# Another order for the first attention: four stages of two key tiles in place of eight of one

## The chip, the cores and the metric

The kernel runs on one core of a Trainium2 chip. The core has TensorE for matrix products (its matmuls are PE in the profile, its weight loads PEld), VectorE (DVE), ScalarE (ACT), GpSimd (POOL) and SyncE (SP, which here issues the DMAs). The engines run side by side, each through its own list of instructions in order, and wait for one another at semaphores. The metric is the device time of one execution in microseconds; lower is better. The median of three runs of the kernel before is 1487.65 us.

## The reference

Two transformer layers over x of shape (2, 1024, 128): a wide attention, a mixture of eight gated experts, a second attention (causal, with a rotary part) and a second mixture. The change is in the first attention:

```python
q = z @ wq @ fcq_w + fcq_b        # 16 heads of 64, z = layernorm(x)
k = z @ wk @ fck_w + fck_b
v = z @ wv @ fcv_w + fcv_b
scores = einsum('bihd,bjhd->bhij', q, k) / 8
attn = softmax(scores, axis=-1)
out = einsum('bhij,bjhd->bihd', attn, v)
return out.reshape(b, n, 1024) @ fco_w + fco_b
```

## The kernel before

The first attention goes through 16 **steps**, numbered 0 to 15. A step handles a pair of heads of one batch. Its 1024 keys are eight key tiles of 128, its 1024 queries two halves of 512. For each key tile `kt` and each half `j` of the queries there is

- a **score unit** (`ST`): four matmuls of 512 columns (L931, L932) that fill one PSUM tile called `pair`; ScalarE turns it into `prob` by an exponential (L680);
- a **value unit** (`PV`, function `product`, L904): the values times `prob`, two fp32 matmuls that the profile shows as four records, summed over the eight key tiles in the PSUM tile `pv`.

GpSimd adds the `prob` of the key tiles up in `psum_k` (L623, L628), for the sums of the softmax. Beside this the step does small jobs, each a letter in the code:

- for the **next** step: `q` twice (the projection of the queries, L854, read by ScalarE at L638 and then by VectorE at L732), `s` sixteen times (the raw scores with queries on the partitions, two matmuls of 64 rows, L863 and L865, of which VectorE takes the maxima at L738), and `m` (the maxima are brought into a row: `mmax` at L742 joins the two halves of the keys, a transpose at L883, then `mrow` at L747, and a DMA from `mrow` into row 0 of the next step's `q2`, L528). The first score unit of a step waits for that DMA (`row_loaded`);
- for the step **before**: `l` (column sums, L888, copied at L751), `r` (reciprocals, L771), `n` (the values times the reciprocals, L775) and `g` (output projection, L893, added at L779).

In steps 0 to 11 a piece of the experts' weights is split as well: VectorE computes two halves of its rest (L812) after all the units of the step and ahead of those of the next one. Steps 12 to 14 carry early parts of the second layer (`R`, `X`, `P`).

All `ST` and all small jobs but `r` and `n` share a ring of three `pair` tiles: a unit on TensorE waits until the tile that was filled three ring places earlier has been read. The order on TensorE, ScalarE and VectorE is the order of `step_script`, which before the change reads the tables `AFTER_SCORES` and `AFTER_VALUES`: for every key tile two `ST`, what the first table says, the two `PV` of the key tile before, what the second table says. So the value units run one key tile behind the scores.

Of the kernel before, what the change touches and what calls it, by code (L numbers as in the profile page):

```python
# [367 lines left out]
def step_units(k_next, k_done):  # L368
# [5 lines left out]

AFTER_SCORES = {
    0: [("q", 0), ("q", 1)],
    1: [("s", 1), ("s", 2)], 2: [("s", 4), ("s", 5)], 3: [("s", 7), ("s", 8)], 4: [("s", 10), ("s", 11)],
    5: [("s", 13), ("s", 14)],
}
AFTER_VALUES = {  # L380
    0: [("s", 0)], 1: [("s", 3), ("l", 0)], 2: [("s", 6), ("X", 0)], 3: [("s", 9), ("r", 0)], 4: [("s", 12)],
    5: [("s", 15)], 6: [("m", 0), ("n", 0), ("R", 0), ("P", 0)], 7: [("g", 0)],
}

# [6 lines left out]
def step_script(n):  # L391

    has = step_units(n + 1 < STEPS0, n > 0) + EARLY.get(n, [])
    out = []
    for kt in range(TT):
        out += [("ST", kt, 0), ("ST", kt, 1)]
        out += [("UNIT",) + u for u in AFTER_SCORES.get(kt, []) if u in has]
        if kt or n:
            out += [("PV", kt - 1, 0), ("PV", kt - 1, 1)]
        out += [("UNIT",) + u for u in AFTER_VALUES.get(kt, []) if u in has]  # L400
    return out
# [45 lines left out]
def l0_attention(nc, m, d):  # L447
    with ExitStack() as ctx:
# [3 lines left out]
        def sem(name):  # L452
            return m.ctx.enter_context(nc.semaphore(name))
# [11 lines left out]
        mx = sb("mx", [P, 2, 2, TT])  # L465
        mmax = sb("mmax", [P, 2, TT])
        tcol = sb("tcol", [2 * TT, P])
# [21 lines left out]
        filled, read = sem("work_filled"), sem("work_read")  # L489
        hi_done, mmax_ready = sem("hi_done"), sem("mmax_ready")  # L490
        st_filled, exp_done, pv_done, ut_ready = sem("st_filled"), sem("exp_done"), sem("pv_done"), sem("ut_ready")
# [20 lines left out]
        def _(sp):  # L512
# [62 lines left out]
            for n in range(STEPS0):  # L575
# [10 lines left out]
                if n:  # L586
                    sums(n - 1, place(n, ("l", 0)))
                if n + 1 < STEPS0:
                    max_rows(n + 1, place(n, ("m", 0)))
                    shift_rows(n + 1)  # L590
            sums(LAST, first_of(STEPS0))
# [40 lines left out]
        def _(act):  # L632
# [27 lines left out]
            for n in range(STEPS0):  # L660
                for what, *rest in step_script(n):
# [3 lines left out]
                    elif what == "PV":  # L665
                        kt, j = rest
                        if kt < 0:
                            keep_product(n - 1, j)
                    else:
# [12 lines left out]
                        if j and kt in (4, 5) and piece_of(n) is not None:  # L682
                            lead_piece(piece_of(n), kt - 4)
                        if j and kt == 2 and n == AT_TURN:

                            act.wait_ge(read, place(PAIRS, ("g", 0)) + 1)
                            act.wait_ge(piece_split, 2 * len(PIECES))
                            nc.scalar.activation(turned[:, :], m.out_t[:, 0:T], ACT.Identity, bias=m.out_bias[:, 0:1]
                                                 ).then_inc(early_act, 1)
                        if j and kt == 6 and n == AT_ROOT:  # L690
                            act.wait_ge(m.aggr_done, NBLK + 2)
                            nc.scalar.activation(m.std0[:, 0:HALF], m.mv[:, 0:HALF, 1], ACT.Sqrt, bias=m.eps[:, 0:1]
                                                 ).then_inc(early_act, 1)
                        if j and kt < 2 and n == AT_LOGITS:

                            act.wait_ge(early_dve, CENTRE)
                            act.wait_ge(read, place(AT_TURN, ("R", 0)) + 1)
                            for t in range(TPB * kt, TPB * (kt + 1)):
# [3 lines left out]
                        if j and kt == 4 and n == AT_LOGITS:  # L702
# [4 lines left out]
                        if j and kt == 0 and n == LAST:  # L707
                            act.wait_ge(early_dve, SHIFTED)
# [6 lines left out]
        def _(v):  # L715
# [8 lines left out]
            def unit(kind, x, u, k):  # L724
# [11 lines left out]
                elif kind == "s":  # L736
                    v.wait_ge(filled, u + 1)
                    nc.vector.reduce_max(mx[:, x % 2, :, x // 2], buf[:, :, :], AX.X).then_inc(read, 1)  # L738
                    if x == S_UNITS - 1:

                        v.wait_ge(read, u + 1)
                        nc.vector.tensor_tensor(mmax[:, :, :], mx[:, 0, :, :], mx[:, 1, :, :], ALU.max  # L742
                                                ).then_inc(mmax_ready, 1)
                elif kind == "m":
                    v.wait_ge(cols_loaded, 16 * (k + 1))
                    v.wait_ge(filled, u + 1)
                    nc.vector.scalar_tensor_tensor(mrow[:, :], buf[0:2 * TT, 0, 0:P], -1.0, tcol[:, :],  # L747
                                                   ALU.mult, ALU.subtract).then_inc(read, 1)
# [96 lines left out]
        def _(pe):  # L845
            def unit(kind, x, u, k):
# [34 lines left out]
                elif kind == "m":  # L881
                    pe.wait_ge(mmax_ready, k + 1)
                    ins = nc.tensor.matmul(buf[0:2 * TT, 0, 0:P], mmax[:, :, :].rearrange("p h t -> p (h t)"),  # L883
                                           m.ident[:, :], start=True, stop=True)
                elif kind == "l":
# [26 lines left out]
            for n in range(STEPS0):  # L912
                for what, *rest in step_script(n):
# [7 lines left out]
                    else:  # L921
# [12 lines left out]
                        ins.then_inc(st_filled, 1)  # L934
            for j in R2:
                product(STEPS0 - 1, TT - 1, j)
            u = first_of(STEPS0)
# [1783 lines left out]
```

## Time and profile before

| | before |
|---|---|
| median of 3 runs | 1487.65 us (1487.17 to 1487.96) |
| the profiled execution | 1486.37 us |
| its span, first to last instruction | 1484.6 us |
| PE busy | 1381.6 us, 93% of the span |
| DVE, ACT, POOL busy | 999.2, 817.5, 863.1 us |
| mean granted clock of TensorE | 0.972 |

The profiled execution is the one that all times of the trace come from; 1.8 us of it lie outside the span. The 16 steps begin at 63.84 us and the last value unit ends at 746.9 us. "Busy" of PE counts matmuls that overlap and have modelled ends, so starts of neighbouring records are a better measure of what a unit costs than the length of one record.

### The profile page before, as it was taken

The numbers are of one execution on the slowest core, as the hardware profiler recorded it, in microseconds if no ns is written. First come the engines' busy times: TensorE is split into PE (matmuls) and PEld (weight loads), VectorE is DVE, ScalarE is ACT, GpSimd is POOL, SyncE is SP. The second block draws the span as 40 slices with busy tenths as digits, with TensorE's granted clock in tenths as the row PEclk, the third lists the DMA queues.
The fourth block names the chain that finished last, engine by engine and source line by source line (L and its number), as shares of the span: only waits on it lengthen the run. The fifth ranks groups of instructions, "written<-read, shape, count | busy, mean of one in ns | idle before, by whom it ended". The sixth has DMA issues, their size and how long they took to land. (4 is left out here: it accounts for less than half of the span.)

```text
span 1484.6 us, 18636 instructions
## 1 busy us (share of the span) xinstructions
PE 1381.6 (93%) x6322; PEld 783.4 (53%) x6322; DVE 999.2 (67%) x1675; ACT 817.5 (55%) x1236; POOL 863.1 (58%) x685
## 2 busy tenths in 40 slices
PE   6699999999999999999978977899999997999998
PEld 5344444444444444544456734454444445787776
DVE  5676777777677777677666678676666725566665
ACT  4244444444444445444545443566776565787776
POOL 0298777777977777787744505455565332344443
PEclk9699999999999999999999997999999998999999
DMA  3110111111011111000050005012111106000000
GB/s 107 33 44 16 58 59 44 58 58 48 26 58 58 51 52 44 15 16 15 26 159 1 1 0 100 15 24 30 21 30 29 30 2 271 1 1 8 8 8 8
DMA packets 32586, 60.59 MB, mean 41 GB/s; under 512 B 9499, under 2 KB 17084, under 8 KB 32348
## 3 DMA queue, kind: packets, MB, share of 16 engines
q1 hardware_dynamic: 32492, 59.40, 14.4%
q8 instruction: 51, 0.84, 0.2%
q14 instruction: 43, 0.35, 0.1%
HBM read 35.13 MB, written 13.89 MB: 33 GB/s over the span
## 5 line engine op out<-in xcount | busy, mean ns | idle before, releaser
L628 POOL TENSOR_TENSOR psum_k<-psum_k,prob 128x1024 f32<-128x1024 f32 x186 | 457.9, 2485 | 46.5 <-ACT prob L680 46.5
L680 ACT ACTIVATE prob<-pair 128x1024 f32<-128x1024 f32 x256 | 250.5, 1025 | 378.7 <-PE pair L932 378.7
L738 DVE TENSOR_REDUCE mx<-pair 128x2 f32<-128x1024 f32 x256 | 305.3, 1222 | 100.0 <-PE pair L865 99.5
L904 PE MATMUL pv<-prob,c_all 128*64 128x512 f32 x1024 | 247.9, 605 | 0.0
L1935 DVE CUSTOM_DVE_ANT_0 l_banks<-l_banks,causal 128x128 f32<-128x128 f32 (+7 forms) x256 | 189.5, 782 | 75.8 <-PE l_banks L1973 74.7
L931 PE MATMUL pair<-qq,ak 128*128 128x512 f32 x512 | 221.5, 433 | 7.1 <-DVE q L732 3.3
L1843 ACT ACTIVATE l_prob<-l_banks 128x1024 f32<-128x1024 f32 (+7 forms) x256 | 155.3, 654 | 111.7 <-PE l_banks L1992 111.0
L932 PE MATMUL pair<-q,kb 128*128 128x512 f32 x512 | 202.4, 395 | 0.0
L2151 POOL TENSOR_TENSOR silu_rest_t<-silu_t,silu_lead_t 128x512 fp32r<-128x512 f32 x74 | 96.4, 1304 | 145.0 <-ACT silu_lead_t L2348 145.0
L1897 POOL TENSOR_SCALAR_AFFINE_SELECT l_prob<-l_prob 128x128 f32<-128x128 f32 x256 | 72.3, 295 | 146.9 <-ACT l_prob L1843 145.3
L623 POOL TENSOR_TENSOR psum_k<-prob 128x1024 f32<-128x1024 f32 x31 | 74.1, 2412 | 118.9 <-ACT prob L680 118.9
L931 PEld LDWEIGHTS pair<-qq,ak 128*128 128x128 f32 x512 | 96.6, 189 | 73.2 <-issue 22.8
L2517 DVE TENSOR_TENSOR silu_t<-silu_t,bank_t 128x512 f32<-128x512 f32 x128 | 88.0, 688 | 64.4 <-ACT silu_t L2339 60.4
L1973 PE MATMUL l_banks<-l_kk,l_qq 128*128 128x512 f32 (+3 forms) x384 | 115.4, 394 | 14.1 <-DMA l_qq<-rounded 4.7
L2339 ACT ACTIVATE silu_t<-bank_t,b_t 128x512 f32<-128x512 f32 x144 | 99.3, 690 | 41.8 <-PE bank_t L951 41.6
L904 PEld LDWEIGHTS pv<-prob,c_all 128*64 128x64 f32 x1024 | 62.1, 136 | 112.6 <-issue 80.6
L863 PE MATMUL pair<-ak,qq 64*128 64x512 f32 x256 | 112.8, 487 | 9.0 <-DVE mx L738 5.0
L1992 PE MATMUL l_banks<-l_qq,l_kk 128*128 128x512 f32 (+3 forms) x384 | 112.1, 385 | 4.2 <-DVE plain L1935 3.2
L865 PE MATMUL pair<-kb,qq 64*128 64x512 f32 x256 | 113.1, 488 | 0.0
L863 PEld LDWEIGHTS pair<-ak,qq 64*128 64x128 f32 x256 | 47.0, 188 | 122.0 <-issue 94.6
L932 PEld LDWEIGHTS pair<-q,kb 128*128 128x128 f32 x512 | 96.9, 189 | 19.8 <-issue 3.3
L1973 PEld LDWEIGHTS l_banks<-l_kk,l_qq 128*128 128x128 f32 x384 | 64.9, 199 | 73.7 <-ACT l_prob L1843 23.6
(318 smaller groups left out, 2276.8 us busy)
## 6 DMA issues: line engine op xcount, KB each, us to landing
plain<-scratch_sums SPq DMA_DIRECT2D x32, 256.0 KB
whole<-in_experts SPq DMA_DIRECT2D x12, 512.0 KB, 5.1
scratch_lead<-rounded SPq DMA_DIRECT2D x12, 512.0 KB, 2.6
scratch_rest<-rounded SPq DMA_DIRECT2D x12, 512.0 KB, 3.9
w_lead_t<-scratch_lead SPq DMA_DIRECT2D x9, 512.0 KB, 6.6
w_rest_t<-scratch_rest SPq DMA_DIRECT2D x9, 512.0 KB, 7.4
l_kk<-rounded SPq DMA_DIRECT2D x16, 256.0 KB, 4.2
l_qq<-rounded SPq DMA_DIRECT2D x16, 256.0 KB, 5.4
```

What stands on the lines that cost most here:

```text
L628: nc.gpsimd.tensor_tensor(total[:, h, :], total[:, h, :], prob[kt % 4][:, h, :], ALU.add).then_inc(summed, 1)
L680: nc.scalar.activation(prob[kt % 4][:, :, ts(j, BLK)], buffer("ST", at)[:, :, :], ACT.Exp, scale=D0 ** -0.5).then_inc(exp_done, 1)
L738: nc.vector.reduce_max(mx[:, x % 2, :, x // 2], buf[:, :, :], AX.X).then_inc(read, 1)
L863: nc.tensor.matmul(buf[:, 0, :], qq[k % 2][0][0:D0, ts(t, P)], m.ak[0:D0, keys], start=True, stop=True)
L865: ins = nc.tensor.matmul(buf[:, 1, :], qq[k % 2][1][D0:P, ts(t, P)], m.kb[D0:P, keys], start=True, stop=True)
L904: ins = nc.tensor.matmul(pv[D0 * h:D0 * (h + 1), ts(j, BLK)], m.c_all[:, TT * (s // PAIRS) + kt, :], prob[kt % 4][:, h, ts(j, BLK)], start ...
L931: nc.tensor.matmul(buf, m.ak[:, keys], qq[n % 2][h][:, ts(j, BLK)], start=True, stop=False)
L932: ins = nc.tensor.matmul(buf, m.kb[:, keys], q2[n % 2][:, h, ts(j, BLK)], start=False, stop=True)
L1843: nc.scalar.activation(prob[kt % 2][:, g, P * kt:T], buffer(item)[:, P * kt - T:], ACT.Exp, scale=SCALE1).then_inc(exp_done, 1)
L1935: ins = nc.vector.tensor_tensor_reduce(scores[:, 0:s_width(t)], scores[:, 0:s_width(t)], hidden, 1.0, -3e38, ALU.add, ALU.max, mx[:, g, t: ...
L1973: ins = nc.tensor.matmul(out[:, lo:end], qq[k % 2][:, g, ts(t, P)], kk[k % 2][:, g, lo:end], start=True, stop=True)
L1992: ins = nc.tensor.matmul(buf[:, at:at + end - lo], kk[n % 2][:, g, ts(kt, P)], qq[n % 2][:, g, lo:end], start=True, stop=True)
```

## The change

One table, `STAGES`, replaces the two. A step is now four stages, each with the four `ST` of two key tiles, the small jobs among them, and the four `PV` of the two key tiles of the stage before. The `PV` of key tiles 6 and 7 so fall in the first stage of the next step (after the last step: at its end). Of the small jobs, the two `q` and all `s` stand among or around the score units. The two halves of the maxima are no longer joined on VectorE at L742: `m` now is two transposes on TensorE, and VectorE joins them with a maximum over two in PSUM (`top`). On SyncE, the row of shifts is issued ahead of the row of maxima.

```diff
-AFTER_SCORES = {
...
-AFTER_VALUES = {
...
+STAGES = [
+    ["ST", ("q", 0), "ST", "ST", ("s", 0), "ST", ("q", 1), ("s", 1), ("s", 2),
+     "PV", "PV", "PV", "PV", ("l", 0)],
...
+    [("s", 12), "ST", "ST", ("s", 13), "ST", ("s", 14), "ST", ("s", 15),
+     "PV", "PV", ("m", 0), "PV", ("g", 0), "PV", ("R", 0), ("P", 0)],
+]
+STRIDE = TT // len(STAGES)
...
-    for kt in range(TT):
-        out += [("ST", kt, 0), ("ST", kt, 1)]
-        out += [("UNIT",) + u for u in AFTER_SCORES.get(kt, []) if u in has]
-        if kt or n:
-            out += [("PV", kt - 1, 0), ("PV", kt - 1, 1)]
-        out += [("UNIT",) + u for u in AFTER_VALUES.get(kt, []) if u in has]
+    for stage, items in enumerate(STAGES):
+        at = {"ST": 2 * STRIDE * stage, "PV": 2 * STRIDE * (stage - 1)}
+        for item in items:
+            if item in at:
+                if at[item] >= 0 or n:
+                    out.append((item, at[item] // 2, at[item] % 2))
+                at[item] += 1
+            elif item in has:
+                out.append(("UNIT",) + item)
...
                 if n + 1 < STEPS0:
+                    shift_rows(n + 1)
                     max_rows(n + 1, place(n, ("m", 0)))
-                    shift_rows(n + 1)
...
-                    if x == S_UNITS - 1:
-
-                        v.wait_ge(read, u + 1)
-                        nc.vector.tensor_tensor(mmax[:, :, :], mx[:, 0, :, :], mx[:, 1, :, :], ALU.max
-                                                ).then_inc(mmax_ready, 1)
                 elif kind == "m":
...
-                    nc.vector.scalar_tensor_tensor(mrow[:, :], buf[0:2 * TT, 0, 0:P], -1.0, tcol[:, :],
+                    top = buf[0:2 * TT, 1, 0:P]
+                    nc.vector.reduce_max(top, buf[0:2 * TT, 0, 0:2 * P].rearrange("p (a n) -> p n a", a=2), AX.X
+                                         ).then_inc(top_ready, 1)
+                    v.wait_ge(top_ready, k + 1)
+                    nc.vector.scalar_tensor_tensor(mrow[:, :], top, -1.0, tcol[:, :],
                                                    ALU.mult, ALU.subtract).then_inc(read, 1)
...
-                    pe.wait_ge(mmax_ready, k + 1)
-                    ins = nc.tensor.matmul(buf[0:2 * TT, 0, 0:P], mmax[:, :, :].rearrange("p h t -> p (h t)"),
-                                           m.ident[:, :], start=True, stop=True)
+                    pe.wait_ge(read, place(k - 1, ("s", S_UNITS - 1)) + 1)
+                    for half in R2:
+                        ins = nc.tensor.matmul(buf[0:2 * TT, 0, ts(half, P)],
+                                               mx[:, half, :, :].rearrange("p h t -> p (h t)"), m.ident[:, :],
+                                               start=True, stop=True)
...
-            for j in R2:
-                product(STEPS0 - 1, TT - 1, j)
+            for kt in range(TT - STRIDE, TT):
+                for j in R2:
+                    product(LAST, kt, j)
```

On TensorE, around the end of a step (`m` is the row with `ident`, `g` the one with `g_all`, `q` the ones with `w_all`), before:

```order
L904 MATMUL pv<-prob,c_all 64x512 x4
L893 MATMUL pair<-on,g_all 128x512 x2
L931 MATMUL pair<-qq,ak 128x512
L932 MATMUL pair<-q_0,kb 128x512
...
L932 MATMUL pair<-q_0,kb 128x512
L854 MATMUL pair<-aq,w_all 128x512 x8
L904 MATMUL pv<-prob,c_all 64x512 x4
L863 MATMUL pair<-ak,qq 128x512
L865 MATMUL pair<-kb,qq 128x512
L931 MATMUL pair<-qq,ak 128x512
```

and now, from `m` of one step to the first two projections of the next:

```order
L887 MATMUL pair<-ident,mx 16x128 x2
L909 MATMUL pv<-prob,c_all 64x512 x2
L898 MATMUL pair<-on,g_all 128x512 x2
L909 MATMUL pv<-prob,c_all 64x512 x2
L936 MATMUL pair<-qq,ak 128x512
L937 MATMUL pair<-q_0,kb 128x512
...
L857 MATMUL pair<-aq,w_all 128x512 x4
...
L866 MATMUL pair<-ak,qq 128x512
L868 MATMUL pair<-kb,qq 128x512
L936 MATMUL pair<-qq,ak 128x512
```

The first `s` of the step stood behind eight score matmuls, both projections and two value units; it now stands behind three score units and the first projection, with no value unit in between, and a score unit follows it.

On TensorE inside a step (the third of the four stages), now:

```order
L866 MATMUL pair<-ak,qq 128x512
L868 MATMUL pair<-kb,qq 128x512
L936 MATMUL pair<-qq,ak 128x512
L937 MATMUL pair<-q_1,kb 128x512
L936 MATMUL pair<-qq,ak 128x512
L937 MATMUL pair<-q_1,kb 128x512
L866 MATMUL pair<-ak,qq 128x512
L868 MATMUL pair<-kb,qq 128x512
L936 MATMUL pair<-qq,ak 128x512
L937 MATMUL pair<-q_1,kb 128x512
```

Before, eight score matmuls of a key tile stood together with two `s` behind them; here one `s` stands alone between two groups of four.

On VectorE, from the transpose of the maxima to the first maxima of the next step, before:

```order
L742 TENSOR_TENSOR mmax<-mx 128x16
L747 SCALAR_TENSOR_TENSOR mrow<-pair,tcol 16x128
L775 TENSOR_TENSOR on<-plain 128x1024
L779 TENSOR_TENSOR plain<-pair,plain 128x1024
L812 TENSOR_TENSOR rounded<-whole,rounded 128x512 x2
L732 SCALAR_TENSOR_TENSOR q_0<-pair,q_bias,qq 64x512 x4
L738 TENSOR_REDUCE mx<-pair 128x2 x4
```

and now:

```order
L747 TENSOR_REDUCE pair<-pair 16x128
L750 SCALAR_TENSOR_TENSOR mrow<-pair,tcol 16x128
L782 TENSOR_TENSOR plain<-pair,plain 128x1024
L815 TENSOR_TENSOR rounded<-whole,rounded 128x512 x2
L736 SCALAR_TENSOR_TENSOR q_0<-pair,q_bias,qq 64x512 x2
L742 TENSOR_REDUCE mx<-pair 128x2
L736 SCALAR_TENSOR_TENSOR q_0<-pair,q_bias,qq 64x512 x2
L742 TENSOR_REDUCE mx<-pair 128x2 x2
```

The two halves of the weights' rest (L812, now L815) still stand between `g` and the first projection; `on` (unit `n`) has moved up to the end of the third stage.

## Rows read from the trace of the kernel before

**Rows 1.** Busy time of each engine in the stretch of one step, with the clock

```profile
core 0: us, PE busy (x) PEld busy (x) DVE busy (x) ACT busy (x) POOL busy (x), PEclk, DMA share, GB/s
322.00:365.00 43.00, 42.58 (x183) 20.62 (x182) 31.24 (x29) 19.94 (x26) 33.94 (x15) 1.00 0.16 51
```

**Rows 2.** PE in order of time, from step 6's beginning: start us, us, engine, line

```profile
317.20 1.98 PE L893 MATMUL pair<-on,g_all 128*128 128x512 f32 x4
318.62 0.80 PE L931 MATMUL pair<-qq,ak 128*128 128x512 f32 x1
...
324.65 0.49 PE L863 MATMUL pair<-ak,qq 64*128 64x512 f32 x1
...
325.35 0.50 PE L931 MATMUL pair<-qq,ak 128*128 128x512 f32 x1 [0.20 <-DVE q L732]
...
326.69 0.50 PE L931 MATMUL pair<-qq,ak 128*128 128x512 f32 x1 [0.15 <-DVE q L732]
...
327.95 0.50 PE L863 MATMUL pair<-ak,qq 64*128 64x512 f32 x1
...
330.90 1.06 PE L888 MATMUL pair<-psum_k,ones 128*32 128x512 f32 x8
331.90 0.50 PE L931 MATMUL pair<-qq,ak 128*128 128x512 f32 x1
...
361.63 0.80 PE L931 MATMUL pair<-qq,ak 128*128 128x512 f32 x1
```

**Rows 3.** PE in order of time, one repeat of the inner pattern

```profile
333.95 0.50 PE L863 MATMUL pair<-ak,qq 64*128 64x512 f32 x1
...
334.29 0.41 PE L863 MATMUL pair<-ak,qq 64*128 64x512 f32 x1
...
334.64 1.94 PE L904 MATMUL pv<-prob,c_all 128*64 128x512 f32 x8
336.51 0.49 PE L863 MATMUL pair<-ak,qq 64*128 64x512 f32 x1
...
336.93 0.50 PE L931 MATMUL pair<-qq,ak 128*128 128x512 f32 x1
337.26 0.39 PE L932 MATMUL pair<-q,kb 128*128 128x512 f32 x1
...
338.65 0.40 PE L932 MATMUL pair<-q,kb 128*128 128x512 f32 x1
338.98 0.50 PE L863 MATMUL pair<-ak,qq 64*128 64x512 f32 x1
```

**Rows 4.** PE in order of time, around the transpose of the maxima

```profile
312.97 0.39 PE L883 MATMUL pair<-ident,mmax 128*16 128x128 f32 x2
313.29 0.50 PE L931 MATMUL pair<-qq,ak 128*128 128x512 f32 x1
```

**Rows 5.** DVE in order of time, at the beginning of the same step

```profile
319.22 1.23 DVE L779 TENSOR_TENSOR plain<-pair,plain 128x1024 f32<-128x1024 f32 x1 [3.45 <-PE pair L893]
320.36 3.47 DVE L812 TENSOR_TENSOR rounded<-whole,rounded 128x512 fp32r<-128x512 f32 x2
323.87 2.77 DVE L732 SCALAR_TENSOR_TENSOR q<-pair,q_bias,qq 64x512 fp32r<-64x512 f32 x4
326.67 1.23 DVE L738 TENSOR_REDUCE mx<-pair 128x2 f32<-128x1024 f32 x1
```

**Rows 6.** Line L812 by itself: durations in ns (least, median, most)

```profile
L812 DVE TENSOR_TENSOR rounded<-whole,rounded x24: 678/2204/2868, 101.0 to 581.3; 128x512 fp32r<-128x512 f32 x24
```

**Rows 7.** POOL in order of time, across the beginning of the step

```profile
312.31 10.37 POOL L628 TENSOR_TENSOR psum_k<-psum_k,prob 128x1024 f32<-128x1024 f32 x4 [0.33 <-ACT prob L680]
329.02 2.36 POOL L623 TENSOR_TENSOR psum_k<-prob 128x1024 f32<-128x1024 f32 x1 [6.34 <-ACT prob L680]
```

**Rows 8.** ACT in order of time, the projections of the same step

```profile
321.99 2.42 ACT L638 ACTIVATE qq<-pair,q_bias 128x512 fp32r<-128x512 f32 x4
```

**Rows 9.** All engines in order of time, ahead of step 0's first scores

```profile
60.89 0.59 PE L883 MATMUL pair<-ident,mmax 128*16 128x128 f32 x2 [2.90 <-DVE mmax L742]
...
63.84 0.77 PE L931 MATMUL pair<-qq,ak 128*128 128x512 f32 x1 [2.37 <-issue]
```

More of the change, by code:

```diff
@@ L372, in step_units @@
             + [("l", 0), ("r", 0), ("n", 0), ("g", 0)] * k_done)
-AFTER_SCORES = {
[L376 to L379, printed above, removed]
-AFTER_VALUES = {
-    0: [("s", 0)], 1: [("s", 3), ("l", 0)], 2: [("s", 6), ("X", 0)], 3: [("s", 9), ("r", 0)], 4: [("s", 12)],
-    5: [("s", 15)], 6: [("m", 0), ("n", 0), ("R", 0), ("P", 0)], 7: [("g", 0)],
-}
+STAGES = [
[8 rows of a table added]
+]
+STRIDE = TT // len(STAGES)
 STATISTICS_BEHIND = (3, 8)
@@ L465, in l0_attention @@
         mx = sb("mx", [P, 2, 2, TT])
-        mmax = sb("mmax", [P, 2, TT])
         tcol = sb("tcol", [2 * TT, P])
@@ L489, in l0_attention @@
         filled, read = sem("work_filled"), sem("work_read")
-        hi_done, mmax_ready = sem("hi_done"), sem("mmax_ready")
+        hi_done, top_ready = sem("hi_done"), sem("top_ready")
         st_filled, exp_done, pv_done, ut_ready = sem("st_filled"), sem("exp_done"), sem("pv_done"), sem("ut_ready")
@@ L666, in _ @@
                         kt, j = rest
-                        if kt < 0:
+                        if kt == -1:
                             keep_product(n - 1, j)
@@ L683, in _ @@
                             lead_piece(piece_of(n), kt - 4)
-                        if j and kt == 2 and n == AT_TURN:
+                        if j and kt == 3 and n == AT_TURN:
                             act.wait_ge(read, place(PAIRS, ("g", 0)) + 1)
@@ L689, in _ @@
                                                  ).then_inc(early_act, 1)
-                        if j and kt == 6 and n == AT_ROOT:
+                        if j and kt == 7 and n == AT_ROOT:
                             act.wait_ge(m.aggr_done, NBLK + 2)
@@ L693, in _ @@
                                                  ).then_inc(early_act, 1)
-                        if j and kt < 2 and n == AT_LOGITS:
+                        if j and kt in (1, 3) and n == AT_LOGITS:
                             act.wait_ge(early_dve, CENTRE)
                             act.wait_ge(read, place(AT_TURN, ("R", 0)) + 1)
-                            for t in range(TPB * kt, TPB * (kt + 1)):
+                            for t in range(TPB * (kt // 2), TPB * (kt // 2 + 1)):
                                 ins = nc.scalar.activation(normal[:, t, :], m.x[:, t, :], ACT.Identity,
@@ L701, in _ @@
                             ins.then_inc(early_act, 1)
-                        if j and kt == 4 and n == AT_LOGITS:
+                        if j and kt == 5 and n == AT_LOGITS:
                             act.wait_ge(read, place(AT_LOGITS, ("X", 0)) + 1)
@@ L706, in _ @@
                             nc.scalar.copy(m.early_x[:, 0, :], xt[:, :]).then_inc(early_act, 1)
-                        if j and kt == 0 and n == LAST:
+                        if j and kt == 1 and n == LAST:
                             act.wait_ge(early_dve, SHIFTED)
```

4 rows, old and new, of the table STAGES are left out of this document.

## Prediction

> **What bounds the kernel now.** I read the busy times of one step first, because a step repeats 16 times and the change touches nothing outside the steps. Of 43.00 us TensorE is busy 42.58, GpSimd 33.94, VectorE 31.24, ScalarE 19.94, at granted clock 1.00, that is 2.4 GHz [rows 1]. TensorE has no room; what the change is worth is what it does to the time between starts of TensorE's records. So I then read TensorE in order of time. Step 6 begins at 318.62 and step 7 at 361.63: 43.01 us [rows 2]. In it the reader is to see three things. First, score matmuls follow each other at (338.65 - 337.26) / 6 = 0.232 us, but a run of eight takes 338.98 - 336.93 = 2.05, not 1.85: every run of scores that stands between units of another shape costs 0.20 extra, half where it begins (0.33 to the second record), half where it ends [rows 3]. Second, an `s` costs 0.34 or 0.35 in a pair behind scores and 0.42 behind values; four value records are half of 1.87 and cost nothing extra inside a run [rows 3]; `l` costs 1.00 [rows 2]; `m` 0.32 [rows 4]; `g` 1.87 (four records at twice the pace of the value records; its row and the next scores together take 2 x 1.87). Third, the only waits are at the start of the step: the `s` at 324.65 takes 0.70 instead of 0.42, and the run of scores behind it 2.60 instead of 2.05, both because the ring tiles of the projections are not yet read by VectorE [rows 2]. That is 0.28 + 0.55 = 0.83 us a step, with the restarts.
>
> Then VectorE and GpSimd at that place. `g` is read at 319.22, the rest of a weight piece is asked for at 320.36 and takes 3.47, and the first projection can be read only from 323.87 [rows 5]. One half of the rest takes 0.68 alone and up to 2.87 otherwise [rows 6]. GpSimd's four additions end at 312.31 + 10.37 = 322.68 [rows 7]; 0.68 behind that is 323.4, about where the first half ends (320.36 + 2.87 = 323.2). So this VectorE instruction, which reads two SBUF tensors, waits for the end of a GpSimd instruction. The page "SBUF — State Buffer" of the Trainium skill (section "SBUF: two separate sides") has the rule: the two share a port pair which one holds for a whole instruction. The trace agrees (0.68 against 2.87). By that rule each half can lose up to one GpSimd addition; it makes the rival B below.
>
> **The change part by part.** I price TensorE's list of a full step without waits.
> - Stage 1: one run of 16 records (ST q ST ST) 3.71 + 0.20 = 3.91; `s` alone 0.34; a run of eight 2.05; two `s` 0.70; four PV 3.74; `l` 1.00. Sum 11.74.
> - Stage 2: `s` 0.42; 2.05; `s` 0.34; 2.05; two `s` 0.70; 3.74. Sum 9.30.
> - Stage 3: `s` 0.42; 2.05; `s` 0.34; a run of four 0.93 + 0.20 = 1.13; 0.34; 1.13; 0.70; 3.74. Sum 9.85.
> - Stage 4: 0.42; 2.05; 0.34; 1.13; 0.34; 1.13; last `s` 0.35; PV PV 1.87; `m` with a second transpose 0.32 + 0.23 = 0.55; PV 0.94; `g` 1.87; PV 0.94. Sum 11.93.
> Together 42.82, against 43.01 - 0.83 = 42.18 before: **+0.64 us a step**. Where it comes from: ten runs of scores pay the 0.20 where seven paid it, +0.23 for the transpose, less 0.30 because fewer `s` stand behind values, plus 0.1 of edges. An `s` between two score runs is not in the trace (six a step now). Below: 0.234, the bare pace of one record, if its weights load behind the scores; above: 0.42, as behind values. I take 0.34, the nearest row: the first of a pair behind scores. The bounds move the step by -0.6 and +0.5.
>
> The page "TensorEngine Tiling (Array Packing)" of the Trainium skill, section "Key Properties", says a change of tiling mode drains the engine. By that rule more changes of shape are pure loss; a step goes from 29 runs to 32, and at about 0.1 us a change it gives +0.3, where my sum of rows (with the transpose and fewer `s` behind values) gives 0.64. I keep the rows.
>
> **The waits.** The 0.83 go: the second key tile's scores no longer come three ring places behind a projection that VectorE has not read. Late next is the first `s`: its ring tile is that of projection 0. Before, that tile was free 325.35 - 317.20 = 8.15 us after `g` began [rows 2]. Now TensorE reaches the `s` at 1.87 + 0.94 + 3.91 = 6.72 after `g` begins. With VectorE's list as it was, the wait is 1.43. But it hangs on when GpSimd lets the rest through. The last two key tiles' scores now end some 6.7 and 3.7 us ahead of `g` (before 6.1 and 1.9), so its last additions, which run without a break, end about 0.6 earlier: wait 8.15 - 0.6 - 6.72 = **0.83**. Bounds: none, if GpSimd is done before the rest is asked for; 3.2, if both halves wait. Behind that `s` nothing else waits: VectorE needs at most 1.23 for each `s` [rows 5] and score units of 0.93 stand between them, and value runs of 3.74 us clear the rest. So in steps 2 to 12 the waits balance, and each of these 11 steps is **0.64 longer: +7.0 us**.
>
> Edges. Steps 13 and 14 have no weight piece and waited for nothing; now the chain of projection 0 decides alone: filled at 1.98, two ScalarE parts of 0.6 (2.42 / 4) [rows 8] from 2.3 on, VectorE's second part to 4.4, against 3.9 for TensorE: 0.5, so +1.1 each, **+2.2**. Step 1 is the same, and its first scores also wait for the row of maxima: `m` to scores took 2.95 when nothing else was in between [rows 9]; with a second transpose and a reduction (nearest rows: 16x128 at 0.28 here, below that of an `s`; I take 0.3) it is 3.4, and step 0 has no `g`, so only 0.55 + 1.87 = 2.4 covers it: 1.0. In later steps `g` adds 1.87 and the row comes 0.9 early. Step 1: **+2.0**. Step 0 has no values in its first stage to hide VectorE's five `s` and two projections: one wait of some 2.5 in place of 1.4, plus 0.64: **+1.8**. Step 15 has four runs of scores where it had eight, -0.8, but more of its values come behind the last scores, where `g` and the sums used to be covered: **0**, between -0.8 and +0.8.
>
> At no price: the missing `mmax` (VectorE did it beneath two value units), the exchanged DMAs on SyncE (the row of shifts, 8 KB, needs nothing of this step and now stands ahead of the waiting one; it lies beneath stage 4), `on` and the sums' DMAs (three stages apart as before), and GpSimd, which needs 14 x 2.36 = 33 us of the 43 [rows 7].
>
> **Sum:** 7.0 + 2.2 + 2.0 + 1.8 + 0 = **+13.0**. The profiled execution (1486.37) becomes 1499.4; it lies 1.3 below the median of the runs, and the same addition to 1487.65 gives **1500.6 us**.
>
> **Rivals.**
> A, **the new order wins**: an `s` between scores costs the bare 0.234 (-0.6 a step) and GpSimd is done in time, so the 0.83 are simply gained. Then a full step is 0.8 shorter: -9, edges +4: 1483. For it: GpSimd has 9 us to spare a step; against it: its additions at the end of a step ran on without a break, and every change of shape in the rows costs something. It needs both; with one alone the time is about 1492. Chance 0.11.
> B, **both halves of the rest wait** for an addition each (or the lone `s` costs 0.42): the wait is up to 2.3 us longer, by one addition in some steps 1.5, or +0.5 for the `s`: 11 x 1 on top, 1509 to 1516. For it: the first half waited almost a full addition before. Chance 0.14.
> C, **nothing to measure**: half of A, with the wait at 0 and the `s` at 0.30: -0.3 a full step and the edges; 1486 to 1490. Chance 0.07.
> D, the row of maxima is late in every step: it needs 0.9 us more than the rows give; then +0.5 a step over my sum, 1508. Chance 0.04.
> The forecast itself, 1491 to 1508: chance 0.64.
>
> A measurement of this kernel can tell 0.2% (3 us) from no change. Faster 0.11, within it 0.07, slower 0.82. The range that should hold the time 8 in 10 is 1490 to 1512; it leaves out A and the far end of B.
>
> **What would show it.** In the profile after: full steps 43.3 to 44.2 us apart; the first record of a lone `s` and the next scores 0.34 apart; no wait on L732's successor before the second key tile's scores, but one of 0.4 to 1.5 us before the first `s` of each of steps 2 to 12; the first half of the rest still 2 us or more; a wait of about 1 us before step 1's scores. The prediction is wrong if steps 2 to 12 are shorter than 43.01, or if TensorE waits anywhere else in them for over 0.5 us.

## The result and the profile after

| | before | after |
|---|---|---|
| median of the runs | 1487.41 us (4 runs) | 1509.95 us (4 runs, 1508.62 to 1512.79) |
| ratio | | 1.0154, 95% interval 1.0137 to 1.0172 |
| profiled execution, its span | 1486.37, 1484.6 us | 1509.54, 1507.8 us |
| start of step 0's scores | 63.84 us | 63.83 us |
| end of the last value unit | 746.9 us | 769.5 us |
| what follows it in the span | 737.8 us | 738.3 us |

The median rose by 22.5 us. In the profiled executions the span grew by 23.2 us, of which 22.7 lie in the 16 steps of the first attention and 0.5 behind them. A full step (2 to 11) takes 44.37 us where it took 43.03; with step 12 that is 11 x 1.34, or 14.8 us. Step 0 is 3.4 longer and step 1 2.4, steps 13 and 14 together 2.3, step 15 0.2 shorter: 22.7 in all.

The busy times of one step, over a window one microsecond longer than that of [rows 1]:

```profile
330.00:374.00 44.00, 42.90 (x184) 20.63 (x183) 29.18 (x29) 20.29 (x24) 33.32 (x15) 1.00 0.16 49
```

TensorE's busy time went up by 0.3 us only, at the same clock; its idle time, 0.4 us before, is now 1.1. VectorE is busy 2 us less, but its busy time holds its waits for GpSimd as well, as shown below. So the longer step has to be looked for between starts of records. Here is the first stage of step 6 after the change, TensorE in order of time; it answers to [rows 2]:

```profile
326.80 1.98 PE L898 MATMUL pair<-on,g_all 128*128 128x512 f32 x4
328.71 1.08 PE L909 MATMUL pv<-prob,c_all 128*64 128x512 f32 x4
329.72 0.50 PE L936 MATMUL pair<-qq,ak 128*128 128x512 f32 x1
...
334.09 0.49 PE L866 MATMUL pair<-ak,qq 64*128 64x512 f32 x1 [0.41 <-DVE q L736]
334.10 0.49 PE L868 MATMUL pair<-kb,qq 64*128 64x512 f32 x1
334.52 0.51 PE L936 MATMUL pair<-qq,ak 128*128 128x512 f32 x1
...
337.27 3.65 PE L909 MATMUL pv<-prob,c_all 128*64 128x512 f32 x16
340.85 1.06 PE L893 MATMUL pair<-psum_k,ones 128*32 128x512 f32 x8
341.85 0.49 PE L866 MATMUL pair<-ak,qq 64*128 64x512 f32 x1
```

The reader is to see three things: the first `s` waits 0.41 us for projection 0; alone between scores it takes 334.52 - 334.09 = 0.43; and the four value units take 340.85 - 337.27 = 3.58, less than twice the 1.87 of [rows 3]. The last stage of the same step:

```profile
361.40 0.50 PE L936 MATMUL pair<-qq,ak 128*128 128x512 f32 x1
...
364.20 0.50 PE L866 MATMUL pair<-ak,qq 64*128 64x512 f32 x1 [0.69 <-DVE mx L742]
...
364.63 0.51 PE L936 MATMUL pair<-qq,ak 128*128 128x512 f32 x1
...
365.77 0.50 PE L866 MATMUL pair<-ak,qq 64*128 64x512 f32 x1
...
366.20 0.50 PE L936 MATMUL pair<-qq,ak 128*128 128x512 f32 x1
...
367.32 0.49 PE L866 MATMUL pair<-ak,qq 64*128 64x512 f32 x1
...
367.75 1.94 PE L909 MATMUL pv<-prob,c_all 128*64 128x512 f32 x8
369.62 0.61 PE L887 MATMUL pair<-ident,mx 128*16 128x128 f32 x4
370.16 1.08 PE L909 MATMUL pv<-prob,c_all 128*64 128x512 f32 x4
371.17 1.98 PE L898 MATMUL pair<-on,g_all 128*128 128x512 f32 x4
373.08 1.08 PE L909 MATMUL pv<-prob,c_all 128*64 128x512 f32 x4
374.09 0.50 PE L936 MATMUL pair<-qq,ak 128*128 128x512 f32 x1
```

Ahead of `s` 13 TensorE waits 0.69 us for VectorE's read of `s` 12 (the run of scores takes 2.80, not 2.05). That wait is new, and the prediction did not have it. VectorE in order of time shows what the read of `s` 12 was behind:

```profile
358.39 1.22 DVE L742 TENSOR_REDUCE mx<-pair 128x2 f32<-128x1024 f32 x1
359.52 3.48 DVE L778 TENSOR_TENSOR on<-plain 128x1024 f32<-128x1024 f32 x1
362.93 1.21 DVE L742 TENSOR_REDUCE mx<-pair 128x2 f32<-128x1024 f32 x1
```

`on` (unit `n`) took 2.09 us before and now takes 3.48. GpSimd, in order of time; the view is cut to the two additions that touch this time:

```profile
359.55 5.68 POOL L632 TENSOR_TENSOR psum_k<-psum_k,prob 128x1024 f32<-128x1024 f32 x2
```

An addition begins at 359.55, 0.03 us behind `n`, and the two additions last 5.68 us where two take 4.7: `n` stood aside for a whole addition, then ran in about 1.1 us, and the second addition stood aside for `n`. The weights' rest, which waited in that manner before [rows 6], no longer does: of its 24 halves only the first two, at 106.0 and 107.9 us, took over 0.76 us. The line by itself:

```profile
L815 DVE TENSOR_TENSOR rounded<-whole,rounded x24: 678/749/2889, 106.0 to 596.8; 128x512 fp32r<-128x512 f32 x24
```

What the first `s` waits for is seen on VectorE, in the first stage of step 6:

```profile
329.96 1.35 DVE L815 TENSOR_TENSOR rounded<-whole,rounded 128x512 fp32r<-128x512 f32 x2
332.61 1.43 DVE L736 SCALAR_TENSOR_TENSOR q<-pair,q_bias,qq 64x512 fp32r<-64x512 f32 x2 [1.29 <-ACT qq L642]
```

The rest of the weights is done at 331.3, and VectorE then stands idle for 1.29 us, until ScalarE has read projection 0. So the rest no longer holds that `s` up.

Ahead of step 1's scores the row of maxima is late, as forecast:

```profile
107.89 0.50 PE L936 MATMUL pair<-qq,ak 128*128 128x512 f32 x1 [0.81 <-DMA q<-mrow]
```

Step 0 differs in one thing more, the granted clock of TensorE (the third figure from the end), before and after:

```profile
63.84:104.56 40.72, 39.63 (x163) 20.33 (x163) 27.24 (x24) 19.11 (x22) 28.46 (x12) 0.96 0.04 14
63.83:107.89 44.06, 40.93 (x156) 22.09 (x156) 24.64 (x24) 19.55 (x22) 30.89 (x14) 0.89 0.04 13
```

The clock starts at 1.2 GHz in both. It rose to 2.4 GHz 3.2 us into step 0 before the change and 5.8 us into it after, and there it fell to 1.2 GHz once more for 3.4 us, behind two waits of TensorE of 1.56 and 0.76 us. In e7 below it did not fall behind the same two waits, so what made it fall is not shown. The price can be estimated from starts of records: the first 16 took 6.55 us where they took 5.42, and the run of eight scores at the second fall took 3.62 where it takes 2.06 at 2.4 GHz. That is some 2.7 us of step 0's 3.4.

### The profile page after: what moved, and what is told of

It is laid out like the page before. It is cut to its first block and busy times, and to the rows that moved or that the text cites. A ratio compares the mean times of both kernels' runs of the same rounds, so it can differ in the third digit from the quotient of the medians.

```text
span 1507.8 us, 18700 instructions
## 1 busy us (share of the span) xinstructions
PE 1396.0 (93%) x6354; PEld 792.2 (53%) x6354; DVE 976.5 (65%) x1675; ACT 822.5 (55%) x1236; POOL 857.5 (57%) x685
## 5 line engine op out<-in xcount | busy, mean ns | idle before, releaser
L632 POOL TENSOR_TENSOR psum_k<-psum_k,prob 128x1024 f32<-128x1024 f32 x186 | 452.6, 2471 | 67.0 <-ACT prob L684 66.6
L684 ACT ACTIVATE prob<-pair 128x1024 f32<-128x1024 f32 x256 | 253.6, 1026 | 359.6 <-PE pair L937 359.2
L742 DVE TENSOR_REDUCE mx<-pair 128x2 f32<-128x1024 f32 x256 | 307.6, 1222 | 116.9 <-PE pair L868 116.4
L909 PE MATMUL pv<-prob,c_all 128*64 128x512 f32 x1024 | 240.2, 601 | 0.0
L866 PE MATMUL pair<-ak,qq 64*128 64x512 f32 x256 | 120.9, 499 | 23.1 <-DVE mx L742 14.1
L909 PEld LDWEIGHTS pv<-prob,c_all 128*64 128x64 f32 x1024 | 65.2, 136 | 123.5 <-issue 112.7
L868 PE MATMUL pair<-kb,qq 64*128 64x512 f32 x256 | 120.7, 499 | 0.0
```

What stands on the lines that cost most here:

```text
L632: nc.gpsimd.tensor_tensor(total[:, h, :], total[:, h, :], prob[kt % 4][:, h, :], ALU.add).then_inc(summed, 1)
L684: nc.scalar.activation(prob[kt % 4][:, :, ts(j, BLK)], buffer("ST", at)[:, :, :], ACT.Exp, scale=D0 ** -0.5).then_inc(exp_done, 1)
L866: nc.tensor.matmul(buf[:, 0, :], qq[k % 2][0][0:D0, ts(t, P)], m.ak[0:D0, keys], start=True, stop=True)
L868: ins = nc.tensor.matmul(buf[:, 1, :], qq[k % 2][1][D0:P, ts(t, P)], m.kb[D0:P, keys], start=True, stop=True)
L909: ins = nc.tensor.matmul(pv[D0 * h:D0 * (h + 1), ts(j, BLK)], m.c_all[:, TT * (s // PAIRS) + kt, :], prob[kt % 4][:, h, ts(j, BLK)], start ...
```

## The experiments

"Steps" are the mean lengths of steps 2 to 11 in us, all at the full clock; they are steadier than the medians, since the part behind the attention, in which no kernel differs, takes 734.6 to 741.1 us in the profiled executions, and the part ahead of it 63.1 to 65.6. The mean granted clock of the part behind was 0.97 where that part was shortest (e4 and e5_again) and 0.95 where it was longest (e1 and e8).

| kernel | median us | ratio to before, 95% | steps |
|---|---|---|---|
| e1_n_between | 1503.08 | 1.0111 (1.0091 to 1.0131) | 43.61 |
| e2_q_first | 1511.09 | 1.0171 (1.0145 to 1.0197) | 44.27 |
| e3_after_small | 1500.44 | 1.0088 (1.0063 to 1.0113) | 43.61 |
| e4_before_small | 1474.14 | 0.9928 (0.9901 to 0.9955) | 42.24 |
| e5_rest_around_g | 1478.94 | 0.9934 (0.9920 to 0.9948) | 42.21 |
| e5_again | 1476.74 | 0.9940 (0.9927 to 0.9952) | 42.21 |
| e6_new_m | 1488.45 | 1.0012 (1.0001 to 1.0023) | 43.04 |
| e7_old_m | 1513.13 | 1.0169 (1.0153 to 1.0185) | 44.62 |
| e8_fewer_runs | 1497.85 | 1.0064 (1.0048 to 1.0079) | 43.14 |
| e9_joined_end | 1476.76 | 0.9932 (0.9919 to 0.9945) | 41.86 |
| e10_joined_but_last | 1472.24 | 0.9897 (0.9881 to 0.9914) | 41.88 |

**e1_n_between**, on the changed kernel:

```diff
-    [("s", 7), "ST", "ST", ("s", 8), "ST", ("s", 9), "ST", ("s", 10), ("s", 11),
-     "PV", "PV", "PV", "PV", ("n", 0)],
+    [("s", 7), "ST", "ST", ("s", 8), "ST", ("s", 9), "ST", ("s", 10), ("n", 0), ("s", 11),
+     "PV", "PV", "PV", "PV"],
```

> The changed kernel with one entry of its table moved: the product `n` on VectorE comes between the reads of `s` 10 and 11 instead of behind both. Nothing moves on TensorE. Theory (the 0.69 us wait of TensorE ahead of `s` 13 in every step comes from `n`, which asks for SBUF just behind the start of a GpSimd addition and so holds VectorE 3.48 us instead of about 1.1 plus a short wait): `n` is asked for about 1.2 us earlier, in the middle of an addition, lasts 2.0 to 2.5 us, and the wait ahead of `s` 13 goes; 0.75 us in each of steps 1 to 13, about 10 us off 1510, so 1499 to 1501. Rival (VectorE is simply behind because of its own work; the order within it does not matter): the wait stays at 0.5 to 0.7 and the time within 2 us of 1510.

Steps fell by 0.76 us and the wait ahead of `s` 13 is gone. The attention ended 9.1 us earlier (760.4); the median fell by 6.9 and so missed the expected range by 2, as the part behind it took 2.7 more in the profiled execution. Step 14 became 1.1 us longer: TensorE there waits 1.26 us for VectorE ahead of a score unit. VectorE in order of time:

```profile
352.33 1.23 DVE L742 TENSOR_REDUCE mx<-pair 128x2 f32<-128x1024 f32 x1 [0.35 <-PE pair L868]
353.48 2.28 DVE L778 TENSOR_TENSOR on<-plain 128x1024 f32<-128x1024 f32 x1
355.68 2.34 DVE L742 TENSOR_REDUCE mx<-pair 128x2 f32<-128x1024 f32 x2
```

No work was taken away: `n` is 1.2 us shorter because it asks in the middle of an addition, waits for its end and then goes first, and no longer asks where the next addition goes ahead of it. The rival, by which the order within VectorE does not matter, is out.

**e2_q_first**, e1 with projection 0 ahead of the first score unit:

```diff
-    ["ST", ("q", 0), "ST", "ST", ("s", 0), "ST", ("q", 1), ("s", 1), ("s", 2),
+    [("q", 0), "ST", "ST", "ST", ("s", 0), "ST", ("q", 1), ("s", 1), ("s", 2),
```

> As e1_n_between, and the projection 0 stands ahead of the first score unit of a step instead of behind it. Theory (the first `s` of a step waits 0.41 us for the chain scores, exponential, projection on ScalarE, VectorE, and not for the weight piece): that wait goes, 0.46 us in each of steps 1 to 14, and the wait of 0.8 for the row of maxima at step 1 goes as well because the projection covers it: 7 us below e1, near 1493. Rival (the weight piece on VectorE sets the wait, as the prediction had it): at most 0.2 us a step, 1 to 3 us below e1.

Neither expectation came true: steps grew by 0.65. TensorE in order of time:

```profile
329.29 1.20 PE L857 MATMUL pair<-aq,w_all 128*128 128x512 f32 x4
...
333.22 0.51 PE L936 MATMUL pair<-qq,ak 128*128 128x512 f32 x1 [0.89 <-DVE q L736]
```

The theory had overlooked the ring. The tile of projection 0 comes back to the third unit behind it, which was `s` 0 and is now a score unit that stands earlier. Moving a unit up moved its reader's deadline up too. The rival was right in part: in step 13, which has no weight piece, that wait is 0.38 us, and in steps 2 to 12 it is 0.84 to 0.91. VectorE's rest of the weights is asked for 1.0 us ahead of the end of GpSimd's last addition, not 0.2 as in the changed kernel; it takes 2.18 us and is followed by the read of projection 0 without a pause:

```profile
329.52 2.18 DVE L815 TENSOR_TENSOR rounded<-whole,rounded 128x512 fp32r<-128x512 f32 x2
331.73 1.43 DVE L736 SCALAR_TENSOR_TENSOR q<-pair,q_bias,qq 64x512 fp32r<-64x512 f32 x2
```


**e3_after_small** and **e4_before_small** leave most of GpSimd's additions out (the sums of the softmax then cover key tiles 0 and 1 in full and 64 columns of the others):

```diff
-                            nc.gpsimd.tensor_tensor(total[:, h, :], total[:, h, :], prob[kt % 4][:, h, :],
+                            nc.gpsimd.tensor_tensor(total[:, h, 0:64], total[:, h, 0:64], prob[kt % 4][:, h, 0:64],
```

> The changed kernel with GpSimd's additions of key tiles 2 to 7 cut to 64 of 1024 columns; so the sums of the softmax leave most of the keys out. Every wait and semaphore stays. Theory (GpSimd's instructions hold up VectorE's two-operand ones): `n` falls from 3.48 to about 1.1 us, the wait ahead of `s` 13 goes, 0.75 us a step, 1498 to 1500. The wait ahead of the first `s` stays at 0.41. Rival (GpSimd has no part in it): 1508 to 1511.

> The kernel before with GpSimd's additions of key tiles 2 to 7 cut to 64 of 1024 columns; so the sums of the softmax leave most of the keys out. Theory (the first half of the weights' rest waits for GpSimd's last addition and so keeps the ring tiles of both projections from TensorE): that half falls from 2.87 to about 0.7 us and TensorE's waits at the start of steps 2 to 12, 0.83 us each with the restarts, go: 8 to 10 us faster, 1478 to 1480. Rival (the waits come from the projections' own chain through ScalarE and VectorE): steps stay at 43.02 and the time within 2 us of 1487.4.

Both theories hold for the steps. In the changed kernel `n` took 1.22 us and steps were 43.61, exactly as in e1, with the first `s` still waiting 0.41. In the kernel before, TensorE's waits at the start of the step went and steps fell by 0.79. The medians fit less well: e3 lies 0.4 us above its range and e4 4 us under its own. In e4's profiled execution the attention took 9.9 us less than before, which is what was forecast, and the part behind it 3.2 us less at a higher granted clock (0.97 against 0.96). The weights' rest there, L812 by itself:

```profile
L812 DVE TENSOR_TENSOR rounded<-whole,rounded x24: 669/683/686, 101.0 to 571.2; 128x512 fp32r<-128x512 f32 x24
```

The most of it was 2868 ns in [rows 6] and is 686 here. GpSimd's instructions are the cause, and TensorE's only waits in steps 2 to 12 of the kernel before were theirs.

**e5_rest_around_g**, on the kernel before (`rest_of_piece` takes the halves that it is to do):

```diff
                 for kind, x in units:
+                    if kind == "g" and piece_of(done + 1) is not None:
+                        rest_of_piece(done + 1, 0)
                     unit(kind, x, base + seen, done if kind in "lrng" else ahead)
...
-                    rest_of_piece(piece_of(n))
+                    rest_of_piece(piece_of(n), *((1,) if n else R2))
```

> The kernel before, with the first half of the weights' rest (VectorE) ahead of the read of `g` instead of behind it; the second half stays behind it. TensorE's order is untouched. Theory (the 0.8 us of waits at the start of steps 2 to 12 of the kernel before is GpSimd's hold on the rest): the first half now waits in time in which VectorE had nothing to do, VectorE reaches projection 0 up to 2 us earlier, the waits go, steps 2 to 12 fall from 43.02 to 42.2 to 42.4: 7 to 9 us faster, 1478 to 1480. Rival (a half asked for earlier just waits longer and now delays the read of `g`, whose ring tile projection 0 needs): no gain or 1 us a step lost, 1487 to 1498.

> The kernel e5_rest_around_g once more, on the same chip as e9_joined_end, to compare the two and to see whether its gain over the kernel before holds: 8 to 10 us faster than before, steps of 42.20.

Steps of 42.21 in both, the attention ends 9 us earlier (737.8 and 738.1). The gain of 0.6% is clear in both. VectorE in order of time:

```profile
352.66 2.08 DVE L775 TENSOR_TENSOR on<-plain 128x1024 f32<-128x1024 f32 x1
354.67 2.85 DVE L812 TENSOR_TENSOR rounded<-whole,rounded 128x512 fp32r<-128x512 f32 x1
358.20 1.23 DVE L779 TENSOR_TENSOR plain<-pair,plain 128x1024 f32<-128x1024 f32 x1 [0.69 <-PE pair L896]
359.35 0.97 DVE L812 TENSOR_TENSOR rounded<-whole,rounded 128x512 fp32r<-128x512 f32 x1
```

The first half still lasts 2.85 us, but in time in which VectorE waited for `g` before; 0.69 us of idling are left. This shows that the 0.83 us of waits could be won back without any new order on TensorE.

**e6_new_m**, the kernel before with the new join of the maxima alone:

```diff
-                    pe.wait_ge(mmax_ready, k + 1)
-                    ins = nc.tensor.matmul(buf[0:2 * TT, 0, 0:P], mmax[:, :, :].rearrange("p h t -> p (h t)"),
-                                           m.ident[:, :], start=True, stop=True)
+                    pe.wait_ge(read, place(k - 1, ("s", S_UNITS - 1)) + 1)
+                    for half in R2:
+                        ins = nc.tensor.matmul(buf[0:2 * TT, 0, ts(half, P)],
+                                               mx[:, half, :, :].rearrange("p h t -> p (h t)"), m.ident[:, :],
+                                               start=True, stop=True)
```

> The kernel before with only the new way of joining the maxima (two transposes on TensorE, a maximum over two in PSUM on VectorE, no `mmax`); order of work and DMAs as before. Theory (it costs TensorE one more transpose, 0.22 us a step in 15 steps, and frees nothing that TensorE waits for there): 3.3 us slower, 1490 to 1491. Rival (without `mmax`, which waited for GpSimd, GpSimd or VectorE get ahead and the rest of the weights is no longer late): up to 0.8 us a step off, 1482 or less.

Neither came true: the median is 0.4 us above that of the runs of the kernel before made beside it (1488.03), and a full step takes 43.04 for 43.03. `m` takes 0.54 instead of 0.32 in all steps, but of steps 1 to 13 only steps 1 and 13, which had no wait for a projection, are longer by it (0.22 and 0.21). In the full steps the 0.22 is taken back from the wait at the start: the time to projection 0's tile counts from `g`, and the first half of the rest took 2.66 us where it took 2.87. The theory had the size of the term right and missed that a wait absorbs it.

**e7_old_m**, the changed kernel with the old join (the edit of e6 the other way round, in the changed kernel):

```diff
-                    pe.wait_ge(read, place(k - 1, ("s", S_UNITS - 1)) + 1)
-                    for half in R2:
+                    pe.wait_ge(mmax_ready, k + 1)
...
```

> The changed kernel with the old way of joining the maxima (`mmax` on VectorE, one transpose). Theory (in the new order only two value units, 1.87 us, lie between the last `s` and `m`; the read of that `s` ends 1.8 us behind its start, so `mmax`, which can wait a whole GpSimd addition, comes late): TensorE waits 0.3 to 2.3 us ahead of `m`, less 0.22 for the transpose saved: 1 to 30 us slower, most likely near 1525. Rival (`mmax` finds GpSimd's addition just ending): 3 us faster, 1507.

Steps are 44.62, 0.25 longer than those of the changed kernel: inside the expected range and far from its middle. TensorE in order of time:

```profile
367.75 1.94 PE L909 MATMUL pv<-prob,c_all 128*64 128x512 f32 x8
369.97 0.38 PE L888 MATMUL pair<-ident,mmax 128*16 128x128 f32 x2 [1.18 <-DVE mmax L747]
370.28 1.08 PE L909 MATMUL pv<-prob,c_all 128*64 128x512 f32 x4
```

In that step `m` waits 1.18 us for `mmax`, and the wait ahead of `s` 13 is absent; in the step before it is 0.41 and 0.67. The two waits trade with each other: where `m` waits 1.18 us, `mmax` took 1.59 us and `on` 1.22; in steps 5 and 11, where `s` 13 waits, `mmax` took 0.82 and `on` 3.47. That it depends on where in GpSimd's addition each of the two is asked for is argued from these lengths. So the new `m` does earn its second transpose in the new order, by little.

**e8_fewer_runs**, e1 with another last stage:

```diff
-    [("s", 12), "ST", "ST", ("s", 13), "ST", ("s", 14), "ST", ("s", 15),
-     "PV", "PV", ("m", 0), "PV", ("g", 0), "PV", ("R", 0), ("P", 0)],
+    [("s", 12), "ST", "ST", ("s", 13), "ST", "ST", ("s", 14), ("s", 15),
+     "PV", "PV", "PV", ("m", 0), ("g", 0), "PV", ("R", 0), ("P", 0)],
```

> As e1_n_between, and the last stage has its score units in two pairs, its last two `s` together, and three value units together ahead of `m`: one run of scores and one of values fewer on TensorE. Theory (a change of shape has a fixed price on TensorE: 0.20 a run of scores, 0.16 a run of values, 0.16 more for two lone `s` than for a pair): 0.5 us less in each of steps 1 to 14, 43.1 instead of 43.61, 1495 to 1496. Rival (what it saves turns into waits, since VectorE reads the last two `s` 1.13 us apart and ring tiles come back later, or the row of maxima comes late for the next step): 1501 to 1506.

Steps fell from 43.61 to 43.14, 0.47 of the 0.5 forecast, with the same matmuls. The last stage, TensorE in order of time:

```profile
362.14 0.50 PE L866 MATMUL pair<-ak,qq 64*128 64x512 f32 x1
...
362.47 0.42 PE L866 MATMUL pair<-ak,qq 64*128 64x512 f32 x1
...
362.82 2.79 PE L909 MATMUL pv<-prob,c_all 128*64 128x512 f32 x12
365.55 0.61 PE L887 MATMUL pair<-ident,mx 128*16 128x128 f32 x4
```

The price of a change of shape is thus shown by taking changes away, not only read. The median, 1497.85, is 5.2 us under e1's and 2 us above the forecast. The part behind the attention does not account for that, as it took 741.0 us in e1 and 741.1 here. In the profiled executions what was lost lies ahead of step 1: step 0 began 2.2 us later and took 1.2 us longer, as the row of maxima came 1.67 us late for step 1's scores where it came 0.81 late. So the rival was right for that one step.

**e9_joined_end** puts what was learned into e5: at the end of each step of the kernel before, the score units of key tiles 6 and 7 together, `m`, four value units together.

```diff
-    for kt in range(TT):
+    for kt in range(TT - 2):
...
+    out += [("ST", kt, j) for kt in (TT - 2, TT - 1) for j in range(2)]
+    out += [("UNIT",) + u for u in [("m", 0)] if u in has]
+    out += [("PV", kt, j) for kt in (TT - 3, TT - 2) for j in range(2)]
+    out += [("UNIT",) + u for u in [("n", 0), ("R", 0), ("P", 0), ("g", 0)] if u in has]
```

> e5_rest_around_g with what the four stages gained taken over where no `s` has to be placed: at the end of a step of the kernel before, the four score units of key tiles 6 and 7 stand together, then `m`, then the four value units of key tiles 5 and 6, then `g`. Theory (a run of scores costs 0.20 and a run of values 0.16 whatever its length, and here no ring tile is late because ScalarE reads a score unit in 0.93 us): one run of each fewer in every step, 0.36 us off 42.20, so 41.85, and 5 to 6 us faster than e5: 1473 to 1474. Rival (the joined `mmax`, the row of maxima or the product `n` come late, or GpSimd's last additions slip behind the rest of the weights again): waits of 0.4 us or more a step come in, and the time is 1478 to 1487.

Steps were 41.86, as the theory said, yet the time was that of e5: step 15 took 42.4 us to the last value unit instead of 36.6. TensorE, and VectorE ahead of it, in that step:

```profile
731.48 2.05 PE L900 MATMUL pair<-on,g_all 128*128 128x512 f32 x2 [3.64 <-DVE on L779]
```

```profile
725.35 2.70 DVE L794 TENSOR_TENSOR psum_k<-psum_k,prob 128x1024 f32<-128x1024 f32 x1 [0.60 <-ACT prob L684]
727.98 3.35 DVE L779 TENSOR_TENSOR on<-plain 128x1024 f32<-128x1024 f32 x1
```

In step 15 VectorE adds a half of the sums itself, and the order of the units had put `n` behind its last addition. Both instructions are also longer than alone (1.23 us for VectorE's additions just before, 1.22 for `on` in e3), with GpSimd busy throughout.

**e10_joined_but_last** keeps step 15 in its old order:

```diff
-    for kt in range(TT - 2):
+    for kt in range(TT - 2 if n < STEPS0 - 1 else TT):
...
+    if n == STEPS0 - 1:
+        return out
```

> e9_joined_end with step 15 in its old order. Theory (e9 gained 0.35 us in each step and lost it in step 15, where `n` now stood behind VectorE's own addition of key tile 7 and `g` waited 3.6 us for it): steps stay at 41.86, the last value unit comes 36.6 us after step 15 begins instead of 42.4, and the time is 5 to 6 us under e9: 1471. Rival (the end of the last step is set by the sums of the softmax, so that whatever comes earlier waits there): the same as e9, 1476 to 1477.

1472.24 us, ratio 0.9897 (0.9881 to 0.9914): 1% faster than the kernel before and 2.5% than the changed one. Step 15 takes 36.5 us to the last value unit, the attention ends at 731.1. The end of step 6, TensorE in order of time; it answers to [rows 4]:

```profile
344.94 0.50 PE L872 MATMUL pair<-ak,qq 64*128 64x512 f32 x1
...
345.37 0.50 PE L940 MATMUL pair<-qq,ak 128*128 128x512 f32 x1
...
349.25 0.39 PE L892 MATMUL pair<-ident,mmax 128*16 128x128 f32 x2
349.57 3.65 PE L913 MATMUL pv<-prob,c_all 128*64 128x512 f32 x16
353.15 1.98 PE L902 MATMUL pair<-on,g_all 128*128 128x512 f32 x4
```

Sixteen score records in 3.88 us and sixteen value records in 3.58, with no wait. This is what the four stages were after, at the one place of the step where no `s` has to be fitted in.

## Why the prediction was right, and where not

Forecast 1500.6, range 1490 to 1512; measured 1509.95. The sign held, and so did the larger mechanism: the new order changes the shape of TensorE's matmuls more often, and each change costs. The size did not hold. A full step came out 1.34 us longer where 0.64 was forecast, and the time lies outside the 1491 to 1508 that the prediction gave to its own account. It lies in the range of rival B, of whose two conditions one was true (a lone `s` costs 0.42) and the other false (both halves of the rest wait). Of the 1.34 us, TensorE's list without waits makes 0.96, where the prediction had 0.64, and the waits 0.38, where it had none: 0.83 went and 1.21 came. By its own terms (forecast 43.65, measured 44.37):

- **The lone `s`**: 0.34 taken from the first of a pair, 0.43 measured, the upper bound. Six of them and the last `s` (0.35 taken, 0.43): +0.62. This was rival B's value for the term.
- **Value units**: priced as if free of a fixed cost. The runs of 16, 8 and 4 records take 3.58, 1.87 and 1.01: (3.58 - 1.87) / 8 = 0.214 a record and 0.16 a run. Three runs at 3.58 for 3.74, two at 1.01 for 0.94: -0.34. The prediction's "cost nothing extra inside a run" was right, but it doubled and halved the time of a whole run, and with it the fixed cost.
- **Runs of scores** (2.05, 1.13), `m` (0.54), `l` (1.00): as forecast; `g` 0.04 more. e8 shows the prices of the runs.
- **The first `s`**: 0.83 of waiting forecast, 0.46 measured. The step that failed is GpSimd's end. Its last addition ends 3.36 us behind the start of `g` (330.16 against 326.80) where it ended 5.48 behind ([rows 2] and [rows 7]): 2.1 us earlier, of which the prediction had 0.6. The rest begins at 329.96, 0.2 us ahead of that end, so it lasts 1.35 for both halves and waits for next to nothing. What is left is the other chain (scores, ScalarE, VectorE), priced at 0.5 for steps 13 and 14: right there, and it holds in all steps. VectorE's 1.29 us of waiting for ScalarE shows it, and so does e3, in which the wait stays at 0.41 without GpSimd's additions.
- **The wait ahead of `s` 13**: 0.75 with its restart, not forecast at all. The prediction named "`on` and the sums' DMAs (three stages apart as before)" among the edits at no price. That is the step that failed most: `on` had moved from behind `m`, where VectorE then idled 3.45 us [rows 5], to a place where the next `s` starts 1.4 us behind it and needs VectorE, and it is an instruction of the same kind as the rest, whose wait for GpSimd the prediction had just explained. e1 and e3 show the cause from two sides.

Sum: 0.62 - 0.34 + 0.04 - 0.37 + 0.75 = +0.70, of 0.72. The prediction gave as a sign of failure a wait of over 0.5 us elsewhere in the steps, and that is what there was.

The edges: steps 0 and 1 forecast +3.8, measured +5.8; steps 13 and 14 +2.2 and +2.3; step 15 0 and -0.2. The sum for steps 0 and 1 lacks two terms: the clock's 2.7 us in step 0, and the two value units (eight records, some 1.7 us) that leave step 0 while two are added to step 15. That steps 13 and 14 came out right is luck: the prediction gave 1.1 to each, and step 13 became 1.7 longer and step 14 0.6. It also said that these two waited for nothing before; step 14 had waits of 0.96 and 0.30 us for its projections. The wait for the row of maxima ahead of step 1 was 0.81 for 1.0. Rival A (the new order wins) needed the bare 0.234 for a lone `s`, which is out. Rival D's row of maxima is late at step 1 only.

The rule of "SBUF — State Buffer" (Trainium skill, section "SBUF: two separate sides"), one holder of the port pair for a whole instruction, has a larger part in the story than the prediction gave it: the waits of before (e4), the new one (e1, e3) and, as argued, the trade of e7 agree with it. The drain on a change of tiling mode (Trainium skill, "TensorEngine Tiling (Array Packing)", section "Key Properties") agrees with e8, though no run separates the drain from the rest of the 0.20 and 0.16 us.

## What to carry to other kernels

Count changes of matmul shape before regrouping work on TensorE: here each run of scores cost 0.20 us and each run of values 0.16 whatever its length, so joining runs pays (e10) only if it doesn't cut others up. On VectorE, look first at every instruction that reads two SBUF tensors while GpSimd is busy: it can cost nearly a whole GpSimd instruction more (3.48 us for 1.22, beside additions of 2.36), and should stand where nothing is due behind it (e5, 0.6% for one move). And a unit moved within a ring of buffers moves the deadline of another (e2, e9): follow the ring, not only the unit.

## What was not expected of the hardware

- Coming just ahead of GpSimd's next addition did not help. `on`'s record begins 0.03 us ahead of that addition's (359.52 against 359.55), yet the addition ran first. The addition before it ended only at 359.61, so both were asked for while GpSimd still held. Before the change `on` came 1.0 us ahead of such an end (313.68 against 314.69), and there it went first and the next addition waited.
- The steps lock into one phase. `on` took 3.48 us in steps 1 to 12 alike (3481 to 3487 ns), so a wait of 2.3 us that one moved entry makes 1.1 (e1) is paid in every step. It is not a law: in e7 two steps of the twelve, 5 and 11, fell otherwise.
- The part behind the attention, which no kernel changes, took 734.6 to 741.1 us in the profiled executions, and e5 differed from itself by 4.6 us there (739.5 at a granted clock of 0.96, 734.9 at 0.97). Over the 13 profiled executions the part is the longer, by and large, the lower its granted clock; what sets the clock there is not shown. Differences under 3 us between medians are not read as the attention's.
